# A two-layer mixing and quantised-FFN kernel: masked fp32 mixing weights, and a reordered first phase

## The reference, cut to what matters

```python
# layer 0: a small MLP on cond gives 8 softmax weights per batch ...
att = softmax(gelu(gelu(cond @ W0 + b0) @ W1 + b1) @ W2 + b2)      # 64 x 8
agg_w = einsum('bk,koi->boi', att, weight[..., 0])                 # a 64x64 mixing matrix per batch
mixed = einsum('boi,bih->boh', agg_w, x) + (att @ bias_k)[:, :, None]
# ... then a 1024x1024 layer in fp8 with one scale per tensor (maximum of |.|)
x = x + (q8(mixed) @ q8(f0w.T)) * (x_scale * w_scale) + f0b
# layer 1: a grouped 9-tap convolution, then a 4-bit 1024x1024 layer
y = conv(x, convw, groups=4) + (cond @ c_weight.T)[:, :, None] + fside
x = x + y @ ((W_q - zero) * scale).T + f1b
```

## Time and profile before

| | us |
|---|---|
| median of 3 runs (527.1 to 528.81) | 527.64 |
| the profiled execution, its own time | 530.63 |
| its span | 528.8 |
| PE busy | 510.2 |
| DVE busy | 414.1 |
| ACT busy | 244.2 |
| POOL busy | 59.3 |

### The profile page before, as it was taken

One profiled execution on the slowest core, in us unless ns is written; L12 is line 12 of the kernel. 1 busy time (PEld: TensorE's weight loads), 2 busy tenths in 40 slices (PEclk: granted clock), 3 DMA queues, 4 the chain that ended last, 5 costly groups with the idle time before them and its releaser, 6 DMA issues.

```text
span 528.8 us, 9489 instructions
## 1 busy us (share of the span) xinstructions
PE 510.2 (96%) x3480; PEld 284.7 (54%) x3512; DVE 414.1 (78%) x524; ACT 244.2 (46%) x286; POOL 59.3 (11%) x68
## 2 busy tenths in 40 slices
PE   5799999899999999999999999999999999999997
PEld 4444454355555555555555555555555555555563
DVE  7799999877877777777777777777777777777652
ACT  3469898655344444444444444444444444442310
POOL 5266776011000000000000000000000000000000
PEclk9999999999999999999999999999999999999999
DMA  7999591146666666665656565656656666566532
GB/s 220 382 390 403 206 337 55 58 103 134 189 199 187 183 185 184 182 180 180 180 180 180 180 180 180 180 180 180 180 180 180 183 182 180 181 189 190 193 121 79
DMA packets 85651, 100.61 MB, mean 190 GB/s; under 512 B 34468, under 2 KB 67046, under 8 KB 85638
## 3 DMA queue, kind: packets, MB, share of 16 engines
q1 hardware_dynamic: 84610, 99.41, 59.9%
q0 software_dynamic: 656, 0.82, 0.9%
q10 hardware_dynamic: 372, 0.20, 0.1%
HBM read 58.41 MB, written 32.75 MB: 172 GB/s over the span
## 4 chain that ended last, share of the span: by engine, by line
PE 77%; DVE 12%; DMA 4%; issue 3%; SPq 2%; ACT 1%; POOL 1%; ACTq 0%; DVEq 0%; POOLq 0%
PE pair L1181 40%; PE pair L1155 19%; PE pair L1171 15%; DVE stat L804 5%; DMA Y<-in_L_ffn_weight_dram 2%; DMA work<-work 2%; PE pair L1055 1%; DVE work L729 1%; DVE work L819 1%; DVE work L921 1%; DVE Y L819 1%; DVE work L732 1%; PE pair L1145 1%; SPq L336 1%; POOL fixed L489 1%
## 5 line engine op out<-in xcount | busy, mean ns | idle before, releaser
L1181 PE MATMUL pair<-f1T,work 128*128 128x512 f16 x1024 | 231.0, 379 | 0.0
L1181 PEld LDWEIGHTS pair<-f1T,work 128*128 128x128 f16 x1024 | 98.9, 98 | 113.5 <-DVE work L928 0.2
L608 ACT ACTIVATE work<-Y,consts 128x1024 bf16 (+1 forms) x29 | 33.3, 1148 | 185.7 <-DVE work L902 185.7
L921 DVE TENSOR_TENSOR work<-Y,work 128x512 f16<-128x512 f16 (+1 forms) x64 | 71.2, 1119 | 48.0 <-ACT work L641 46.9
L1155 PE MATMUL pair<-f0T,work 128*128 128x512 bf16 x435 | 98.6, 379 | 1.8 <-DMA work<-work 0.3
L1171 PEld LDWEIGHTS pair<-taps,work 128*128 128x128 f16 x1536 | 88.3, 98 | 8.7 <-issue 0.9
L1171 PE MATMUL pair<-taps,work 128*128 128x128 f16 x1536 | 91.2, 219 | 0.6 <-issue 0.5
L934 DVE TENSOR_TENSOR Y<-pair,Y 128x512 f32 (+1 forms) x64 | 43.9, 686 | 44.4 <-PE pair L1181 44.4
L641 ACT CAST work<-Y 128x512 f16 (+1 forms) x64 | 69.6, 1137 | 19.3 <-DVE Y L911 15.6
L1155 PEld LDWEIGHTS pair<-f0T,work 128*128 128x128 bf16 x464 | 45.3, 98 | 55.1 <-DMA work<-work 0.6
L1055 PE MATMUL pair<-Y,work 128*128 128x512 f32 x128 | 61.2, 613 | 0.4 <-ACT Y L581 0.4
(11 more groups left out here) (157 smaller groups left out, 242.4 us busy)
## 6 DMA issues: line engine op xcount, KB each, us to landing
Y<-in_x_dram SPq DMA_DIRECT2D x64, 512.0 KB, 3.9
out_dram<-Y SPq DMA_DIRECT2D x31, 512.0 KB, 3.8
split_rows<-work SPq DMA_DIRECT2D x30, 520.0 KB, 2.6
work<-split_rows SPq DMA_DIRECT2D x30, 520.0 KB, 3.9
Y<-in_L_ffn_weight_dram SPq DMA_DIRECT2D x8, 512.0 KB, 9.0
Y<-in_L_ffn_W_q_dram SPq DMA_DIRECT2D x5, 512.0 KB, 15.1
work<-in_L_ffn_W_q_dram SPq DMA_DIRECT2D x3, 512.0 KB, 15.2
work<-work SPq DMA_DIRECT2D x8, 65.0 KB, 3.9
```

Source lines behind the costliest of these rows:

```text
L921: nc.vector.tensor_tensor(split[:, r, s, 1], v[:, r, :], split[:, r, s, 0], ALU.subtract)\
L1181: last = mm(ps[2 + h][:, :], y1s[n][:, e, k, :], f1T[:, k, h * H:(h + 1) * H], start=False, stop=(e == 1 and k == KT - 1), skip_group_chec ...
```

## The change

The split into bf16 parts and the nine moves go. `att` is repeated eight times along the free axis and transposed to 64 partitions (k, c), then multiplied by a mask `own_c`, so that one fp32 matmul with 512 columns does eight of the old ones: four such matmuls on the unmoved fp32 `weight`. All `keep_clock(12)` and `keep_clock(10)` go. The order of the loads, of DVE's early work and of the tap transposes changes. ScalarE's six placings wait for two semaphores instead of three. The maxima of tiles 0 and 1 move from round 0 in among the steps of the weight scale, whose PE steps go from tiles 0 and 1 to tiles 2 and 3. `scale_w0` moves three tiles later, the turns of the first matrix one tile later, and the last two turns of the second matrix behind the last mixed tile.

```diff
-            return pair[m][par * C:(par + 1) * C, :].rearrange("p (j t b) -> p b t j", t=T, b=NB)[:, b]
+            return pair[m][par * C:(par + 1) * C, :].rearrange("p (q c t b) -> p b t q c", q=2, c=KC, t=T)[:, b]
...
-        groups = [(0, 1)] + [g for r in range(R8) for g in ((3 * r + 1, 2), (3 * r + 3, 1))]
+        groups = [(0, 1), (1, 1), (2, 2)] + [g for r in range(1, R8) for g in ((3 * r + 1, 2), (3 * r + 3, 1))]
...
-        turns0 = {3 * r + 6: r for r in range(R8)}
-        turns1 = {3 * n + 8: n for n in range(KT)}
+        turns0 = {3 * r + 7: r for r in range(R8)}
+        turns1 = {3 * n + 8: n for n in range(KT - 2)}
...
+        turn_order += [("w1", KT - 2), ("w1", KT - 1)]
...
-            for e in range(2):
-                sp.wait_ge(wk_parts, (1, 3)[e])
-                for i in range(3):
-                    sp.dma_start(wkp9[3 * i + e:KP:9, :], wkp[:, e, :]).then_inc(ld["wkp"], 16)
             load_w0(3)
+            load_mixing(0)
+            sp.wait_ge(mbk_zero, 1)
+            for b in range(NB):
+                sp.dma_start(mbk2[0:KR:KC, b * C:(b + 1) * C], cbk).then_inc(ld["mbk"], 16)
             load_w0(4)
-            for b in range(NB):
-                sp.dma_start(mbk2[:, b * C:(b + 1) * C], cbk).then_inc(ld["mbk"], 16)
             load_w0(5)
-            load_mixing(0)
+            load_mixing(1)
...
-                if n == 3:
+                if n == 5:
                     sp.wait_ge(mix_mm, 2)
+                    sp.wait_ge(mlp_mm, 6)
                 load_w1(n)
...
         def _(pool):
+            for b in range(NB):
+                pool.dma_start(convraw[b * C:(b + 1) * C], convw).then_inc(ld["convw"], 16)
...
+            nc.gpsimd.memset(mbk2, 0.0).then_inc(mbk_zero, 1)
...
-            pool.wait_ge(wk_parts, 4)
-            for i in range(3):
-                pool.dma_start(wkp9[3 * i + 2:KP:9, :], wkp[:, 2, :]).then_inc(ld["wkl"], 16)
...
-            act.dma_start(wkf, cwk.rearrange("k (c o) i a -> (k c) (o i a)", c=KC)).then_inc(ld["wk"], 16)
...
+            act.dma_start(wkf, cwk.rearrange("k (c o) i a -> (k c) (o i a)", c=KC)).then_inc(ld["wk"], 16)
...
-                if t == 1:
+                if t == 3:
                     act.wait_ge(zs_mm, 1)
...
-                if t == 2:
+                if t == 5:
                     act.wait_ge(w_step, 2)
-                if t % 3 == 2 and t <= 20:
-                    scale_w0(t // 3 + 1)
+                if t % 3 == 2 and 5 <= t <= 23:
+                    scale_w0(t // 3)
...
+            for n in (KT - 2, KT - 1):
+                keep_w1(n)
             keep_sums(0)
...
-            for n in range(3):
-                clear_mixw(n)
-            dve.wait_ge(ld["wk"], 16)
...
+            clear_mixw(0)
+            clear_mixw(1)
+            dve.wait_ge(ident_made, 1)
+            nc.vector.tensor_reduce(own_c, ident[0:KR, 0:KR].rearrange("p (k c) -> p c k", k=K), AX.X, ALU.add)\
+                .then_inc(own_made, 1)
+            clear_mixw(2)
+            clear_mixw(3)
...
-            largest_w0(0)
             dve.wait_ge(mlp_mm, 4)
             nc.vector.tensor_reduce(nmax, ps[3][0:B, 0:K], AX.X, ALU.max, negate=True).then_inc(mlp_ev, 1)
+            largest_w0(0)
...
+            nc.vector.tensor_scalar(attR.rearrange("p (k c) -> p k c", k=K),
+                                    ex.unsqueeze(2).to_broadcast([B, K, KC]), rinv, None, ALU.mult).then_inc(mlp_ev, 1)
+            dve.wait_ge(mlp_mm, 5)
+            dve.wait_ge(own_made, 1)
+            nc.vector.tensor_tensor(attM, ps[6][0:KR, 256:256 + B].unsqueeze(1).to_broadcast([KR, KC, B]),
+                                    own_c.unsqueeze(2).to_broadcast([KR, KC, B]), ALU.mult).then_inc(mlp_ev, 1)
...
-            for r in range(1, 5):
+            for r in range(1, 4):
                 largest_w0(r)
             place_last()
-            for r in range(5, R8):
+            for r in range(4, R8):
                 largest_w0(r)
             dve.wait_ge(w_red, R8)
             nc.vector.tensor_reduce(w_part, w_rows, AX.X, ALU.max).then_inc(w_red, 1)
...
+            largest_mixed(0)
             dve.wait_ge(w_pe, 1)
             nc.vector.tensor_reduce(w_all, ps[7][0:1, 0:P], AX.X, ALU.max).then_inc(w_red, 1)
+            largest_mixed(1)
...
-                if r == 0:
-                    largest_mixed(0)
-                largest_mixed(2 * r + 1)
+                if r:
+                    largest_mixed(2 * r + 1)
                 largest_mixed(2 * r + 2)
...
-            keep_clock(12)
-            pe.wait_ge(ld["wkp"], 96)
-            pe.wait_ge(ld["wkl"], 48)
-            pe.wait_ge(attp_ev, 1)
+            turned_tap_rows(range(0, 3))
+            pe.wait_ge(ld["wk"], 16)
+            pe.wait_ge(mlp_ev, 8)
             for q in range(4):
-                for j in range(8):
-                    o2 = 8 * q + j
-                    last = mm(ps[q][:, j * B:(j + 1) * B], wkp9[:, o2 * 2 * C:(o2 + 1) * 2 * C],
-                              attpT, start=True, stop=True)
+                last = mm(ps[q][:, :], wkf[:, q * 2 * C:(q + 1) * 2 * C], attM.rearrange("p c b -> p (c b)"),
+                          start=True, stop=True)
                 if q % 2:
                     last.then_inc(mix_mm, 1)
...
+            turned_tap_rows(range(3, R8))
...
-                    if t == 1 and h == 0:
+                    if t == 3 and h == 0:
                         pe.wait_ge(w_red, R8 + 2)
...
-            keep_clock(10)
-            pe.wait_ge(placed_act, 3)
+            pe.wait_ge(placed_act, 2)
...
-                if t == 0:
+                if t == 2:
                     pe.wait_ge(w_red, R8 + 1)
...
-            pe.wait_ge(wT_ev, 2 * KT)
+            for n in (KT - 2, KT - 1):
+                turned1(n)
+            pe.wait_ge(wT_ev, 2 * KT - 2)
...
+            pe.wait_ge(wT_ev, 2 * KT)
             weight_sums(1, range(KT))
```

More of the change, by code:

```diff
@@ L81, in mix_src @@
         def mix_src(m, par, b):
-            return pair[m][par * C:(par + 1) * C, :].rearrange("p (j t b) -> p b t j", t=T, b=NB)[:, b]
+            return pair[m][par * C:(par + 1) * C, :].rearrange("p (q c t b) -> p b t q c", q=2, c=KC, t=T)[:, b]
         def mix_dst(m, par, b):
-            o = b * C + 32 * m + par
-            return mixw[b * C:(b + 1) * C, :, o:o + 31:2]
+            rows = mixw[b * C:(b + 1) * C, :, b * C:(b + 1) * C]
+            return rows.rearrange("p t (c m q o) -> p m o t q c", c=KC, m=2, q=2)[:, m, par]
         def held(eng, value):
@@ L106, in adaln_ffn_kernel @@
         mixw = work[:, 0:T * P].rearrange("p (t m) -> p t m", t=T)
-        KP = 9 * K
-        wkp9 = Y[0:KP, 20 * L:22 * L].bitcast(bf16)
         KC = C // K
         KF = C * C // KC
[L113 to L118, removed]
+        KR = K * KC
+        wkf = work[0:KR, 5 * L:5 * L + KF]
+        attM = work[0:KR, 6 * L:6 * L + KC * B].rearrange("p (c b) -> p c b", c=KC)
         wide_taps = f0T[:, 0, 0:CG * R8 * 4].bitcast(fp32).rearrange("p (c j) -> p c j", c=CG)
@@ L130, in adaln_ffn_kernel @@
         mw2 = mlp[:, 832:840]
-        att = mlp[0:B, 840:848]
-        attT = mlp[0:K, 848:912]
+        attR = mlp[0:B, 848:848 + KR]
+        own_c = mlp[0:KR, 912:912 + KC]
         rowb = mlp[0:1, 976:984]
@@ L137, in adaln_ffn_kernel @@
         convraw = work[:, 9088:9088 + CG * TAPS].rearrange("p (c k) -> p c k", c=CG)
-        mbk2 = f0T[0:K, R8 - 1, 0:2 * P].bitcast(fp32)
+        mbk2 = f0T[0:KR, R8 - 1, 0:2 * P].bitcast(fp32)
         zs = small[:, 7 * P:8 * P]
@@ L220, in adaln_ffn_kernel @@
         mlp_ev = sem("mlp_ev")
-        wk_parts = sem("wk_parts")
+        own_made = sem("own_made")
+        mbk_zero = sem("mbk_zero")
         taps_made = sem("taps_made")
@@ L555, in _ @@
             nc.scalar.activation(ex, ps[3][0:B, 0:K], ACT.Exp, bias=nmax, accum_out=rsum).then_inc(mlp_ev, 1)
[L557 to L560, removed]
             act.wait_ge(mixw_zero, 4)
-            for m, par in ((0, 0), (0, 1), (1, 0)):
+            for m in range(2):
                 act.wait_ge(mix_mm, m + 1)
-                for b in range(NB):
-                    ev = nc.scalar.copy(mix_dst(m, par, b), mix_src(m, par, b))
+                for par in range(2 - m):
+                    for b in range(NB):
+                        ev = nc.scalar.copy(mix_dst(m, par, b), mix_src(m, par, b))
                 ev.then_inc(placed_act, 1)
@@ L741, in clear_mixw @@
                 nc.vector.memset(mixw[:, n * R8:(n + 1) * R8, :], 0.0).then_inc(mixw_zero, 1)
-            for n in range(3):
-                clear_mixw(n)
-            dve.wait_ge(ld["wk"], 16)
[L746 to L752, removed]
+            clear_mixw(0)
[5 more added lines that the diff above has]
+            clear_mixw(3)
+            dve.wait_ge(ld["convw"], 32)
+            dve.wait_ge(tapcols_made, 3)
+            for part in (tapsum, tapsum2):
+                nc.vector.tensor_reduce(part, convraw.rearrange("p c k -> p k c"), AX.X, ALU.add)\
```

(42 more changed lines are left out.)

37 lines of the change are left out of this document (11 added, 26 removed).

## The result

The changed kernel takes 531.67 us in the median of four runs, the kernel before 528.06 beside it: a ratio of 1.007, interval [1.0052, 1.0087], so 3.6 us slower where 2.0 less were forecast. A later repetition gave 1.0045 [1.0028, 1.0062]. It is slower in both, by under 1%.

The account below looks back on a forecast made before the run. The first phase's chain over DVE up to the last maximum was taken to bound, with a fixed chain after. Gains of 0.9 (S), 0.63 (round 0) and 0.54 (end wait) took 527.64 to 525.6 us; range 523.8 to 527.7.

Parts of the forecast that it names:

- block 7: Block 7 of the f0w load in the first phase: forecast to land at 20.3 us instead of 24.1.
- wait of 0.56: End of the first phase: DVE's wait for tile 30 before its maximum, forecast to go, 0.54 in the sum.
- Round 0: First round of the first phase: loses the maxima of tiles 0 and 1; gain 0.63 us, the rest left as a wait.
- the tail: End of the first phase: tiles 29 to 31 follow the turn at once, worth 0.54 us in the sum.
- S: Start of round_offset in round 0, at 28.27 us before; forecast 27.4, 0.9 earlier.
- Placing: Copies of the mixing weights: ScalarE's 0.63 us each, DVE's 0.70; tile 0 starts near 18.5 instead of 21.74.
- Mixing weights, length: Four fp32 matmuls, eight entries on PE: 5.9 us, bounds 4.8 and 6.9, ending at 16.85 against 18.39.
- Weight scale: Steps before round 0: DVE's order binds, PE's transpose is not late, scale ready at 26.2 us against 27.09.
- the clock rises late: Rival: tile 0 and all mixing matmuls run at 1.2 GHz, S becomes 29.3, time 527.5 us; chance 0.14.
- Sum: Whole kernel: 0.9 + 0.63 + 0.54 = 2.07, so 2.0 us less; span 528.8 to 526.8, median 525.6.
- What bounds the kernel now: First phase: chain over DVE to the last maximum at 93.76 us, everything after following in a fixed chain.
- Slower: Rival: tiles 0 to 3 all run at 1.2 GHz, S at 33.0, 3.5 us more, 531.1; chance 0.06.

Follow-up runs that it names:

- after_early1: Changed kernel with block 1's scaling (scale_w0(1)) behind tile 3 instead of tile 5; ratio to the kernel before 1.0054.
- best2: Changed kernel with columns written in runs, weight scale back at tiles 0 and 1, 128-row masked matmuls, unread matmuls between phases and behind tile 0; ratio to kernel before 0.9992.
- after_dense: Changed kernel with rows of weight dealt out so neighbouring columns are written in runs, its loads moved to SP; ratio to the kernel before 1.0011.
- after_rows128: Changed kernel with the four masked matmuls over 128 partitions, the lower 64 zero, instead of 64; ratio to the kernel before 1.0032.
- rows128_fill: after_rows128 with ten unread matmuls of 512 columns in PE's wait before tile 0; ratio to the kernel before 1.0037.

## Why the prediction was wrong

The steps that were right: the masked matmuls start at 10.47 (10.95 forecast), block 7 lands at 9.2 + 10.0 = 19.2 (20.3), the step from round 0 to round 1 is 31.62 to 38.68 = 7.06 (7.07) with POOL holding it, as `after_early1` shows, the end loses its wait of 0.56, and the two turns behind tile 31 are hidden. Round 0 and the tail were to give 1.2 of the 2.0 forecast; from S to the last maximum the changed kernel is in fact 1.5 shorter. The 0.3 more lie in the eight last maxima, and no run shows why.

The rest came out of S, forecast 0.9 earlier and in fact 2.9 later than in the execution shown. These steps failed:

- *Placing*, "ScalarE's copies cost 3.76/6 = 0.63 each". That duration belonged to another target pattern. The change spreads eight neighbours 32 bytes apart where they had been 8; a copy costs 1.09, six of them 2.8 more. I gave no upper bound. Undone, S falls 1.8, of which 0.5 are an earlier start.
- *Mixing weights, length*: 7.16, just above my upper bound of 6.9, and not 5.9. The clock did not rise in them at all.
- *Weight scale*, "Tiles 0, 1, 2 at 1.8 each end by 24.0, so PE's transpose is not late". They began 2.4 later, at 20.9, and took 7.62, not 5.4, since the clock was low in tile 0 and the start of tile 1. The transpose waited 3.6 us for tile 2. This step of the change makes S depend on three tiles where it depended on one; undone, S falls 3.7. The slow clock I had as the rival "the clock rises late", at 0.14. Its condition came true, at S = 29.3 by its sum; the slow copies took it on to 31.2.
- *Sum*, "the difference lies around the profiled execution and doesn't change with this edit". A part of it lay inside: S was 28.3 there and 26.0 to 27.5 in four others. The late landing of block 7 was mostly in that one execution. This alone is 1.6 us (28.27 against a median of 26.7).
- *What bounds the kernel now*, "Everything from the last maximum on follows it in a fixed chain". From the last maximum to the unbroken matmuls it took 36.1 us in five traces (`after` and four that differ little from it), 36.7 to 37.5 in seven others, the one shown of before with 37.3 among them, and 37.7 to 38.7 in the four in which the clock fell between the phases.

The time measured, 531.67, lies beside that of the rival "Slower", 531.1, but this is chance: tiles 0 to 3 were not all slow, about five of their sixteen entries were.

The mends overlap: 1.8 and 3.7 of S alone, 5.0 together, after which DVE's four maxima behind `place_last` bind. Together they bring the time back to the kernel before's (1.0006), so the two steps make the loss, but for the 0.5 us of the earlier start. What is not settled is why the better traces (`best2` has its first phase done 1.4 to 3.5 us before the kernel before's) show no more than 0.0 to 0.5 us in the median. Two things on record bear on it, and neither is shown to be the whole. The time less the span of the first to last instruction is 1.8 to 1.9 us in every run with the old start and 1.8 to 2.5 in those of the changed kernels (2.2 in the median of `best2`), so up to 0.4 lie where no trace reaches. And the traces of the kernel before may be late ones, as said.

## What to carry to other kernels

A step that joins an engine's list behind long work inherits every delay of that work: ask not only when its input is ready, but what stands ahead of it on its engine and how sure that is. When a change keeps a copy's size but alters the steps of its target, the old duration is not its price: measure one such copy first. And if the profiled execution is 3 us from the median of the runs, find out which stretch of it is the late one before building a sum on it. Sort the runs by their granted clock too: here two groups of times were two clocks.

## What the runs showed of the hardware

- Copies of 64x512 fp32 from PSUM to SBUF: 1.08 us on ScalarE and on VectorE with a step of 32 bytes in the target (`after`), 0.62 and 0.70 with 8 bytes (`before`), 0.58 and 0.70 in runs of eight (`after_dense`).
- 7.16 us of unbroken fp32 matmuls over 64 rows left TensorE at 1.2 GHz in six traces of six; the same over 128 rows, half of them zero, ran at 2.4 from the second or third entry on in one trace (3.93 us), and took 4.23 to 6.37 in four others. The Trainium skill ("TensorE: Matmul & The Clock Gate", "Part 1: The HAM clock gate") has the clock follow how busy PE has been. These traces agree only with 128 rows: over 64, PE was as busy and the clock did not rise.
- In `after_rows128` the grant fell in an idle stretch of PE (4.05 us before tile 0), and unread matmuls in it kept the clock in `rows128_fill` (5.42 against 8.03 us for three tiles).
- A VectorE step of 0.43 us that started 0.16 us into a GpSimd product of 1.91 took 2.03 (`after_early1`).
- The granted clock of these traces reads 1.00 from the start, also where the matmuls take 1057 ns and not 592 (`after`, 14 to 17 us); only once it has fallen do the readings show 0.50.
